# A post-norm layer kernel: the clip minimum moves from GpSimd to VectorE, ScalarE's setup work is reordered, and the last chunk's high parts go ahead of the roots

## The reference

```
r = sigmoid(x Wr^T);  k = x Wk^T;  v = x Wv^T
log_decay = log(clip(sigmoid(decay), 1e-7))
scale[t, d] = exp(t * log_decay[d])
cum = cumsum(k*v / clip(scale, 1e-10), over t);  state = cum * scale
y = rmsnorm(r * state, ln_w);  x1 = layernorm(x + y Wo^T)
h = gelu(x1 bw1^T + b1);  out = layernorm(x1 + h bw2^T + b2)
```

## Time and profile before

| | |
|---|---|
| median of 3 runs | 842.73 us (842.6 to 844.2) |
| the profiled execution's own time | 842.26 us |
| its span, first to last instruction | 840.5 us |
| PE busy | 809.7 us, 96% of the span |
| DVE busy | 754.3 us, 90% |
| ACT busy | 678.0 us, 81% |
| POOL busy | 356.5 us, 42% |

### The profile page before, as it was taken

How to read it: one execution, slowest core, us unless ns; L and a number is a source line. 1 busy time by engine, 2 the same in 40 slices (tenths; PEclk the granted TensorE clock), 3 DMA queues, 4 the chain that set the end, 5 groups by cost and what they waited for, 6 DMA issues and landing times.

```text
span 840.5 us, 16849 instructions
## 1 busy us (share of the span) xinstructions
PE 809.7 (96%) x5351; PEld 524.9 (62%) x5351; DVE 754.3 (90%) x1399; ACT 678.0 (81%) x969; POOL 356.5 (42%) x579
## 2 busy tenths in 40 slices
PE   5888999999999999999999999999999999999995
PEld 3455666666666666666666666666666666666553
DVE  4889999999999999999999999999999999999876
ACT  5886888888888888888888888888888888888674
POOL 5684333443333444333344333344433334433444
PEclk9999999999999999999999999999999999999998
DMA  8304535344543443553434554334355343444322
GB/s 247 78 28 101 126 89 93 96 109 115 125 107 92 91 108 100 125 125 83 108 84 103 122 125 107 93 89 110 100 125 125 81 106 88 103 97 101 76 51 75
DMA packets 169845, 86.27 MB, mean 103 GB/s; under 512 B 130144, under 2 KB 165472, under 8 KB 169824
## 3 DMA queue, kind: packets, MB, share of 16 engines
q1 hardware_dynamic: 148304, 52.97, 27.4%
q0 software_dynamic: 4608, 16.78, 10.3%
q10 hardware_dynamic: 16912, 16.26, 5.7%
HBM read 20.45 MB, written 16.78 MB: 44 GB/s over the span
## 4 chain that ended last, share of the span: by engine, by line
PE 85%; DVE 6%; POOL 4%; ACT 2%; issue 2%; DMA 1%; POOLq 0%; ACTq 0%; DVEq 0%; SPq 0%
PE ps_r L355 26%; PE ps_o L473 24%; PE ps_f L428 18%; PE ps_r L428 6%; PE ps_o L382 6%; PE ps_o L387 3%; PE ps_s L362 2%; POOL clip_g L1315 1%; DMA x_in<-in_L_attn_x_dram 1%; DVE hid_lo L957 1%; DMA x_t<-x_st 1%; POOL u_rstd L1246 1%; ACT res L666 0%; DVE state L880 0%; DVE u L906 0%
## 5 line engine op out<-in xcount | busy, mean ns | idle before, releaser
L473 PE MATMUL ps_o<-w2T,hid_hi 128*128 128x256 f16 x992 | 218.8, 273 | 6.1 <-DVE hid_lo L957 5.7
L473 PE MATMUL ps_o<-w2T,hid_lo 128*128 128x256 f16 x992 | 218.8, 273 | 0.0
L355 PE MATMUL ps_r<-x_t,proj_hi 128*128 128x512 f16 x768 | 197.1, 379 | 4.1 <-DVE proj_lo L1038 1.4
L648 ACT ACTIVATE hid<-ps_f,b1c,f_scale 128x512 f32<-128x512 f32 x192 | 145.2, 774 | 50.8 <-PE ps_f L428 45.6
L428 PE MATMUL ps_f<-x_t,w1T 128*128 128x512 f16 x768 | 181.9, 379 | 1.1 <-DMA x_t<-x_st 0.9
L1231 POOL TENSOR_TENSOR y_sqs<-y_sq 128x512 f32<-128x512 f32 x32 | 46.8, 1462 | 300.9 <-ACT y_sq L623 300.9
L957 DVE SCALAR_TENSOR_TENSOR hid_lo<-hid,hid_scale,hid_hi 128x1024 f16<-128x1024 f32 (+1 forms) x136 | 161.0, 1227 | 1.6 <-POOL hid_hi L1256 1.6
L355 PEld LDWEIGHTS ps_r<-x_t,proj_hi 128*128 128x128 f16 x768 | 74.7, 98 | 93.6 <-issue 5.2
L685 ACT ACTIVATE hid_hi<-hid,hid_scale 128x2048 f16<-128x2048 f32 (+2 forms) x70 | 125.7, 1797 | 3.2
L428 PEld LDWEIGHTS ps_f<-x_t,w1T 128*128 128x128 f16 x768 | 75.1, 98 | 79.1 <-DMA x_t<-x_st 1.2
L355 PE MATMUL ps_r<-x_t,proj_lo 128*128 128x512 f16 x384 | 114.2, 379 | 0.0
(11 more groups left out here) (173 smaller groups left out, 1421.2 us busy)
## 6 DMA issues: line engine op xcount, KB each, us to landing
x_in<-in_L_attn_x_dram SPq DMA_DIRECT2D x32, 512.0 KB, 3.8
res<-b_row POOLq DMA_DIRECT2D x32, 512.0 KB, 4.6
out_dram<-res ACTq DMA_DIRECT2D x31, 512.0 KB, 3.1
w_in<-in_L_ffn_w_dram SPq DMA_DIRECT2D x2, 1024.0 KB, 9.9
x_t<-x_st SPq DMA_TRANSPOSE x59, 4.3
b_row<-in_L_ffn_b_dram SPq DMA_DIRECT2D x1, 512.0 KB, 13.6
proj_in<-in_L_attn_Wk_dram SPq DMA_DIRECT2D x1, 256.0 KB, 5.1
proj_in<-in_L_attn_Wv_dram SPq DMA_DIRECT2D x1, 256.0 KB, 5.3
```

What stands on the lines that cost most here:

```text
L355: last = nc.tensor.matmul(ps_r[:, m, :], w[:, m, dc, ec * P:(ec + 1) * P], xx[:, :, dc, :], start=(n == 0), stop=(n == 3 * DC - 1))
L473: last = nc.tensor.matmul(o_tok[:, tt, :], hh[:, hc, tt * P:(tt + 1) * P], w2T[:, :, hc, :], start=(hc == 0 and n == 0), stop=(hc == HC - ...
L648: nc.scalar.activation(hid[:, hc, :], f1_bank[hc % NF], ACT.Gelu, bias=b1c[:, hc:hc + 1], scale=f1_scale[:, hc:hc + 1]).then_inc(s_gelu, 1)
```

## The change

The logarithm is taken right after the sigmoid, and a tiny exponential (`warm`) loads the exponential's table before the squares of the first chunk. VectorE computes min(t * log_decay, -23.03) for the whole table with one instruction per half, 2048 steps each; ScalarE then takes the exponential in place with the bias of 23.03. GpSimd's eight minima are gone, and with them the calls of `clip_min`. ScalarE's prologue is put in another order (all four calls of `clip_table` stand earlier, `signs` of w1 too), VectorE's too (`xl(1, 1)` ahead of `kvs(0, 0, 1)`, `wo_scale` and `wo_split_lo` later, `take_bounds(1, 3)` and `hidden_scale` earlier). PE runs m = 2 of `R(1)` ahead of `sum_bounds(0)`, and waits before `O(1)` until VectorE has read `ps_wmax` (`s_hread`).

At the end, GpSimd makes the high parts of tiles 1, 3, 5, 6 of the last chunk (before: 1, 3, 5, 7), all four ahead of `root_z` of the chunk before it, and VectorE normalises tiles 2 and 3 of the last chunk, with statistics that need no `z_shift` for that half.

```diff
@@ SyncE, last chunk
                     for part in (slice(0, 2), slice(2, 3), slice(3, TT)):
-                        if part.stop < TT:
+                        if part.stop <= TT // 2:
                             sp.wait_ge(s_zout, TT * i + TT + part.stop)
                         else:
-                            sp.wait_ge(s_zlast, 1)
+                            sp.wait_ge(s_zlast, part.stop - TT // 2)
@@ PE prologue
-                R(1, False, looped=False, ecs=(0,), slot=1, ms=range(2))
+                R(1, False, looped=False, ecs=(0,), slot=1)
                 sum_bounds(0, NCH)
-                R(1, False, looped=False, ecs=(0,), slot=1, ms=(2,))
...
                 sum_wmax(ps_wmax[:, 5:6], 5, 1, 6)
+                pe.wait_ge(s_hread, 1)
                 O(1, 1)
@@ ScalarE, setup and prologue
             nc.scalar.activation(dec_c[:, 1, :], dec_c[:, 0, :], ACT.Sigmoid).then_inc(s_setup_a, 1)
-            xsq(0, 0, 0, first=True)
             act.wait_ge(s_setup_v, 1)
             nc.scalar.activation(dec_c[:, 2, :], dec_c[:, 1, :], ACT.Ln).then_inc(s_setup_a, 1)
-            xh(0, 0)
+            act.wait_ge(s_const, 1)
+            nc.scalar.activation(warm[:, :], ones_col[:, :], ACT.Exp)
+            xsq(0, 0, 0, first=True)
...
-                cols = slice(n * CH, (n + 1) * CH)
+                act.wait_ge(s_clip, DC)
                 for dc in range(DC):
-                    nc.scalar.activation(clip_g[:, dc, cols], steps[:, cols], ACT.Exp, bias=log_clip[:, :],
-                                         scale=dec_c[:, 2, dc:dc + 1]).then_inc(s_setup_a, 1)
+                    part = clip_g[:, dc, n * CH:(n + 1) * CH]
+                    nc.scalar.activation(part, part, ACT.Exp, bias=log_clip[:, :]).then_inc(s_exp, 1)
...
+                clip_table(0)
+                xh(0, 0)
                 proj_split_hi(0)
                 proj_split_hi(1)
-                act.wait_ge(s_setup_a, 2)
-                act.wait_ge(s_const, 1)
-                clip_table(0)
+                clip_table(1)
+                clip_table(2)
                 proj_split_hi(2)
                 xsq(1, 0, 1)
                 r_gates(0, 0, (0,))
                 xh(1, 1, slot=1)
+                signs(w1_in, w1_sgn, s_w1_in, s_sgn)
+                xsq(2, 0, 2)
+                r_gates(0, 0, (1,))
                 wo_split_hi()
@@ VectorE, setup, last half and prologue
+            dve.wait_ge(s_const, 1)
+            dve.wait_ge(s_setup_a, 2)
+            for dc in range(DC):
+                nc.vector.tensor_scalar(clip_g[:, dc, :], steps[:, :], dec_c[:, 2, dc:dc + 1], -LOG_CLIP, ALU.mult,
+                                        ALU.min).then_inc(s_clip, 1)
             take_xbound(0, 0)
...
-            def norm2_last_tile(c, j):
-                tt = TT - 1
+            def norm2_last_half(c, j):
                 dve.wait_ge(s_zrstd, c + 2)
-                nc.vector.tensor_scalar(res[j][:, tt, :], res[j][:, tt, :], z_mv[:, tt, 0:1], z_rstd[:, tt:tt + 1],
-                                        ALU.subtract, ALU.mult).then_inc(s_zlast, 1)
+                for tt in range(TT // 2, TT):
+                    nc.vector.tensor_scalar(res[j][:, tt, :], res[j][:, tt, :], z_mv[:, tt, 0:1],
+                                            z_rstd[:, tt:tt + 1], ALU.subtract, ALU.mult).then_inc(s_zlast, 1)
...
                 yl(1, y_second)
                 hidden_bound()
+                hidden_scale()
                 x1l(0)
                 mean_sq(1)
                 scans(2, 2, 0)
-                hidden_scale()
                 residual1(1, 1)
@@ GpSimd
-            def clip_min(n):
-
-                for dc in range(DC):
-                    pool.wait_ge(s_setup_a, 3 + DC * n + dc)
-                    nc.gpsimd.tensor_scalar(clip_g[:, dc, n * CH:(n + 1) * CH], clip_g[:, dc, n * CH:(n + 1) * CH],
-                                            1.0, 1.0, ALU.min, ALU.mult).then_inc(s_clip, 1)
...
                 if left in (2, 3):
-                    for h in (1, 3):
+                    for h in POOL_TILES[left == 2]:
                         hh_odd(i + 1, slice(h, h + 1))
...
                 if left > 1:
                     root_z(i)
-                if left == 2:
-                    for h in (5, 7):
-                        hh_odd(i + 1, slice(h, h + 1))
```

More of the change, by code:

```diff
@@ L186, in postln_layer_kernel @@
         s_winv, s_wscl, s_proj_hi, s_alpha = sem("winv_s"), sem("wscl_s"), sem("proj_hi_s"), sem("alpha_s")
-        s_clip = sem("clip_s")
+        s_clip, s_exp = sem("clip_s"), sem("exp_s")
         s_lnw, s_wo_hi = sem("lnw_s"), sem("wo_hi_s")
@@ L208, in postln_layer_kernel @@
         s_diag, s_arow = sem("diag_s"), sem("arow_s")
-        s_hidden, s_row = sem("hidden_s"), sem("alpha2_row_s")
+        s_hidden, s_hread, s_row = sem("hidden_s"), sem("hidden_read_s"), sem("alpha2_row_s")
         s_xsq, s_xroot = sem("xsq_s"), sem("xroot_s")
@@ L242, in tile_groups @@
             return [slice(h, h + n) for h in range(0, HC, n)]
-        POOL_TILES = [[1, 3], [1, 3, 5, 7]]
+        POOL_TILES = [[1, 3], [1, 3, 5, 6]]
         ACT_TILES = [[h for h in range(HC) if h not in tiles] for tiles in POOL_TILES]
@@ L675, in norm2 @@
                 act.wait_ge(s_zshift, c + 1)
-                for tt in range(TT - 1 if last else TT):
-                    if last and tt == 2:
-                        act.wait_ge(s_zshift, c + 2)
+                for tt in range(TT // 2 if last else TT):
                     nc.scalar.activation(res[j][:, tt, :], res[j][:, tt, :], ACT.Identity,
@@ L762, in prologue @@
                 xh(2, 2, slot=2)
-                signs(w1_in, w1_sgn, s_w1_in, s_sgn)
-                clip_table(2)
+                clip_table(3)
                 r_gates(1, 1, (1,))
@@ L774, in prologue @@
                 x1h(0, 1)
-                clip_table(3)
                 r_gates(2, 2, (1,))
@@ L1096, in hidden_scale @@
                 dve.wait_ge(s_wsum, 5)
-                link(nc.vector.tensor_scalar_max(w_max[:, 5:6], ps_wmax[:, 5:6], TINY))
+                nc.vector.tensor_scalar_max(w_max[:, 5:6], ps_wmax[:, 5:6], TINY).then_inc(s_hread, 1)
+                dve.wait_ge(s_hread, 1)
                 link(nc.vector.reciprocal(w_scl[:, 5:6], w_max[:, 5:6]))
@@ L1106, in prologue @@
                 take_xbound(1, 1)
-                dve.wait_ge(s_clip, 1)
+                dve.wait_ge(s_exp, DC)
                 kvs(0, 0, 0)
                 scans(0, 0, 0)
+                xl(1, 1, slot=1)
+                kvs(0, 0, 1)
                 wo_scale()
-                dve.wait_ge(s_clip, 2)
-                kvs(0, 0, 1)
-                xl(1, 1, slot=1)
+                scans(0, 0, 1)
                 wo_split_lo()
-                scans(0, 0, 1)
                 take_bounds(0, 2)
-                dve.wait_ge(s_clip, 2 * DC)
+                dve.wait_ge(s_exp, 2 * DC)
                 kvs(1, 1, 0)
@@ L1126, in prologue @@
                 ustats(0)
-                dve.wait_ge(s_clip, 3 * DC)
+                take_bounds(1, 3)
+                dve.wait_ge(s_exp, 3 * DC)
                 kvs(2, 2, 0)
-                take_bounds(1, 3)
                 norm1(0, 0, 0)
@@ L1185, in step @@
                     z_last(i, j)
-                    norm2_last_tile(i, j)
+                    norm2_last_half(i, j)
                 if left > 2:
@@ L1280, in root_z_half @@
                 nc.gpsimd.tensor_tensor(z_rstd[:, cols], z_ve[:, cols], neg_half[:, cols], ALU.pow).then_inc(s_zrstd, 1)
-                nc.gpsimd.tensor_scalar(z_neg[:, cols], z_mv[:, cols, 0], -1.0, 1.0, ALU.mult,
-                                        ALU.mult).then_inc(s_zneg, 1)
-                pool.wait_ge(s_zrstd, c + half + 1)
-                pool.wait_ge(s_zneg, c + half + 1)
-                nc.gpsimd.tensor_tensor(z_shift[:, cols], z_neg[:, cols], z_rstd[:, cols],
-                                        ALU.mult).then_inc(s_zshift, 1)
+                if half == 0:
+                    nc.gpsimd.tensor_scalar(z_neg[:, cols], z_mv[:, cols, 0], -1.0, 1.0, ALU.mult,
+                                            ALU.mult).then_inc(s_zneg, 1)
+                    pool.wait_ge(s_zrstd, c + 1)
+                    pool.wait_ge(s_zneg, c + 1)
+                    nc.gpsimd.tensor_tensor(z_shift[:, cols], z_neg[:, cols], z_rstd[:, cols],
+                                            ALU.mult).then_inc(s_zshift, 1)
             nc.gpsimd.memset(ident[:, :], 0.0).then_inc(s_zeroed, 1)
@@ L1328, in prologue @@
                 root_rms(0)
-                clip_min(2)
                 root_u(0)
@@ L1336, in prologue @@
                 unscales(3, 3)
-                clip_min(3)
                 pool.wait_ge(s_ready, 2)
```

5 lines of the change are left out of this document (removed).

## The result

The changed kernel took 840.09 us (median of 17 runs, 838.43 to 843.49), the kernel before 842.70 us (17 runs, beside it): a ratio of 0.9971, 95% interval 0.996 to 0.9982. That is 2.6 us faster; 4.9 us, to 837.8, had been predicted. The profiled execution took 841.13 us (span 839.3, mean granted clock 0.993; before 842.26, 840.5 and 0.997). The same kernel on another chip, twelve runs: 840.40 us, ratio 0.9973 (0.996 to 0.9986).

What follows compares the result with a forecast made beforehand. The prediction took TensorE, busy 700 of 700 us in the loop, as the bound, so only the loop's entry and the end could gain: 2.9 + 2.0 = 4.9 us, from 842.73 to 837.8 us, range 836.2 to 840.2.

Steps and rivals of the forecast that it cites:

- The minima and the table loads: Start of the kernel: VectorE's two minima take 1.35 us each; the table loads ahead of x's squares cost zero.
- the second: Rival: at the start VectorE's minima run at one column per cycle, 1.6 late; gain 3.3, 839.4 us; chance 0.10.
- the fourth: Rival: at the start each table load holds ScalarE for another load's length, 2.6 late; 840.4 us; chance 0.04.
- the slower rival: VectorE's minimum at the start is as slow as GpSimd's was, 13.4 late; 851.2 us; chance 0.03.
- Chunk 1's x and the sum of bounds: Prologue: TensorE's gap of 1.22 us before 24.91 vanishes; `sum_bounds(1)` at 41.66 comes 1.2 earlier (0.8 to 1.6).
- Sum at 68.67 ... 2.9 us earlier: Last low part before the loop, at 68.67: 1.2 + 0.3 + 1.2 + 0.2 = 2.9 us earlier (1.9 to 4.0).
- With GpSimd free the root is done before `hl(0, pairs[0])` ends: 1.20 saved: Before the loop: `norm1(1)` no longer waits 1.20 us for GpSimd's root of chunk 1's variance.
- The third term: Before the loop: `norm1(1)` and the low parts behind it, less stretched by GpSimd, gain 0.2 us (0 to 0.8).
- third rival: A term is not passed on, at VectorE's chain, the loop's entry or `root_z`: gain 2.5, 840.2 us; chance 0.19.
- The wait on `s_hread`: Prologue, before `O(1)`: TensorE waits for VectorE's read, which costs it 0.4 us but does not set 68.67.
- The end: After the loop: TensorE's gap of 1.24 us closes and the last stores come 0.8 earlier, 2.04 together.
- Both just fit; if not, up to 0.3 is lost: At the end: `root_z` and `norm2` of the chunk before end just in time; otherwise up to 0.3 us is lost.

Runs made afterwards that it cites:

- e2: The changed kernel with the end of the kernel before, so only the prologue's changes; 842.09 us, ratio 0.9993 to the kernel before.
- e9: The changed kernel unedited, run once more beside the others on one chip; 840.40 us, ratio 0.9973 to the kernel before.
- e5: e3 plus 16 unused transposes in TensorE's gap before the sum of bounds of chunk 1; 838.31 us.
- e4: The changed kernel plus unused transposes on TensorE, 16 before the sum of bounds of chunk 1 and 36 before the first F2; 839.65 us.
- e6: The changed kernel plus only 16 unused transposes on TensorE before the sum of bounds of chunk 1; 840.33 us.
- e3: The changed kernel with chunk 0's last high part (tiles 6 and 7) made by ScalarE instead of GpSimd in the prologue; 838.19 us.
- e8: e5 with tile 6's high part of the last chunk made by ScalarE instead of GpSimd; 838.65 us.
- e11: e5 with `hidden_scale` back behind the scan of chunk 2 and no wait on `s_hread`; 838.39 us.
- e10: e3 with m = 2 of `R(2)`'s first half moved ahead of the sum of bounds of chunk 1; 839.02 us.
- e12: The changed kernel with chunk 0's last high part and tile 6's high part of the last chunk on ScalarE, no idle work; 837.41 us.
- e1: The kernel before with only the end of the change; 840.77 us, ratio 0.9984 to the kernel before.

## Why the prediction was wrong

*The minima and the table loads: right.* 1.31 us each against 1.35, no gap behind any of three loads, squares of x only late as x was, exponentials hidden. So the second, the fourth and the slower rival are out. The Trainium skill, page "ScalarE: Activation LUTs", section "What ACT_TABLE_LOAD costs", would have a drain of 1380 ns behind each switch: the rows at 3.23 and 4.75 show the next instruction 0.01 to 0.02 us after the load's end.

*Chunk 1's x and the sum of bounds: right in kind, at the low edge.* The 1.22 us gap vanished, and with x in at the same time as before (e2, e9) the sum stands at 40.8 and 40.95 instead of 41.66: 0.8 earlier, 1.2 predicted, 0.8 to 1.6 given. What I did not see is that TensorE came 1.5 us earlier and the sum 0.3, so that its wait grew to 2.09 us.

*The failing step: "Sum at 68.67 ... 2.9 us earlier", and "all that follows ... hangs on the same low parts and moves along".* With x in at the same time as before, the sum moved by 1.1 us (e2), and `F1` of chunk 1 came 0.57 us later. Four things stood in the place of the 2.9.

First, the root of chunk 1's variance. "With GpSimd free the root is done before `hl(0, pairs[0])` ends: 1.20 saved" is a term that failed: GpSimd was free, but VectorE's low part (58.28) had started before the root (58.49), which took 1.93 us instead of 1.03, and `norm1(1)` still waited 0.90. Of the 1.20, 0.30 were saved. e5, with x as in before and neither the slow high part nor a fall, splits the sum: 1.16 up to that low part (57.20 against 58.36; predicted 1.2 + 0.3), 0.30 for the wait (1.2), and 0.77 on VectorE's work from `norm1(1)` to the last low part (0.2), which makes 2.2. The third term was too small by 0.6, so part of the agreement with 2.9 is luck.

Second, the last high part. I let the free GpSimd only shorten VectorE's work (0.2). But with the minima gone it met VectorE in another order. Before, its high part started at 62.77, ahead of VectorE's low parts at 62.95, took 1.24 us, and VectorE was the one stretched. Now VectorE started first, at 62.57, and GpSimd's work, 1.15 us for the pair before it, took 4.14: it ended 0.9 us after VectorE's run of operations with two inputs in SBUF (66.17). The Trainium skill, page "SBUF — State Buffer", section "Who interferes with whom", says that the shared port pair is an exclusive lock and that "Issue order, not op shape, decides who blocks"; both traces agree. GpSimd stayed blocked over three VectorE instructions in a row; in e4, e6 and e9 it came in ahead of the third, took 3.01 us, and VectorE's low part of x1 took 2.06 instead of 1.21. e3 took this out and gained 1.9 us. With it and the first fall out (e5) the last low part is at 66.45, 2.2 earlier than before: that much of the 2.9 was there to be had.

Third, the clock. Gaps that grow while an engine has too little to do are not neutral for TensorE: behind the gaps of 2.09 and 2.38 us it ran at 1.2 GHz, and the second fall alone put 6.04 us between the last low part and `F1` (74.57 - 68.53), where 4.38 (73.05 - 68.67) had been, so 1.66 us lost. That a fall costs TensorE time, e3 against e5 shows for the first gap (2.3 us at `O(1)`, one edit apart); for the second gap it is read from this one comparison. The length of a gap does not decide alone: before, one of 2.93 us at 65.14 had no fall behind it.

Fourth, the transposed x1, which the prediction's third rival named and which I had moving along. In the six kernels with idle work it was the last to arrive (e4 to e8, e11), 5.8 to 8.2 us behind its issue. In e3, e10 and e12 it was not, though no fall came behind the second gap there. In the changed kernel's own profile it landed near 71.6, ahead of 74.57, so the high part and the fall account for the loss without it; in e9 it landed near 75.0, where the products alone would have let `F1` start at 74.2 at full clock. It is a limit close behind, and no more is shown.

*The wait on `s_hread`* cost 0.42 us of TensorE off the path, as said.

*The end: right, somewhat too large.* 2.04 predicted, 1.6 in e1's trace, 1.9 by the medians. From the low-part wait in the loop's last step to z's statistics it gained 0.96 rather than 1.24 (before 22.41 us, e1 21.45). "Both just fit; if not, up to 0.3 is lost": they did not, and 0.28 was, 0.17 of it by the roots (e8); the last stretch gave 0.6, not 0.8.

So the third rival, "a term is not passed on", came nearest, at 840.2 with a chance of 0.19. That its number meets 840.09 so well is in part luck: it had neither the clock nor the 1.18 us gained near the loop's end, without which the changed prologue would have cost 0.6 us instead of giving them. The argument that any shift of the last gap goes through the loop one to one held up to 775 us (1.52 us did, with the wrong sign). But I summed savings on VectorE without asking, at each meeting of two engines, who would now be first.

## What to carry to other kernels

Freed time counts only at the last of several waits: list those that stand within a few us behind the one you remove (here a high part, a transposing transfer, the clock), since each can eat the whole gain. When an engine that shares a port or a transfer path becomes earlier, work out the new order of issue, not only the new durations. And where TensorE is to arrive earlier than its data, count what the clock may take back behind the longer gap (1.7 to 2.3 us here). No remedy for that is shown: one real product moved ahead of the sum moved the gap and the fall with it (e10), and idle work kept the clock but gained no time (e5, e6).
